# A two-way selective scan: y's state sums two pairs later, eight places for C rows, and a forward half's silus in one group

## The reference

```
def _mamba(xf, Win, conv_w, conv_b, Wx, Wdt, bdt, A_log, D, Wout):
    xz = einsum('blc,ec->ble', xf, Win)
    u, z = split(xz, 2)                       # 256 channels each
    u = silu(causal_conv(u, conv_w) + conv_b) # 4 taps
    x_dbl = einsum('bld,ed->ble', u, Wx)      # dt (8), B (16), C (16)
    delta = softplus(dt @ Wdt.T + bdt)
    dA  = exp(delta * A)                      # 16 states a channel
    dBu = delta * B * u
    h = dA_l * h + dBu_l                      # scan along 16384 positions
    y = sum over n of h[n] * C_l[n]
    y = (y + u * D) * silu(z)
    return y @ Wout.T
x_recon = _mamba(x) + flip(_mamba(flip(x)))   # forward and backward
out = silu(group_norm(x_recon)) + x
```

## Time and profile before

| | us |
|---|---|
| median of 3 runs | 10606.26 |
| lowest and highest | 10604.6 and 10616.05 |
| profiled execution | 10616.89 |
| its span, first to last instruction | 10615.1 |
| first scan of the two-way layer starts | 7012.7 |
| its last scan ends | 10526.2 |

### The profile page before, as it was taken

One profiled execution on the slowest core, in us unless ns is written; L12 is line 12 of the kernel. 1 busy time (PEld: TensorE's weight loads), 2 busy tenths in 40 slices (PEclk: granted clock), 3 DMA queues, 4 the chain that ended last, 5 costly groups with the idle time before them and its releaser, 6 DMA issues. The chain is left out here.

```text
span 10615.1 us, 137498 instructions
## 1 busy us (share of the span) xinstructions
PE 9717.4 (92%) x45956; PEld 5177.6 (49%) x45956; DVE 8515.8 (80%) x8102; ACT 8057.9 (76%) x14637; POOL 5905.9 (56%) x2628
## 2 busy tenths in 40 slices
PE   9999999999899999999999999988888888888885
PEld 6767767677444444444444444433333333333332
DVE  7858858578599999999999411159999999999997
ACT  5646646466488888888888555579999998888885
POOL 0000000000288888888888300058989988889885
PEclk9999999999899999999999999989999999999997
DMA  1000000000145555545555100035555555555556
GB/s 41 0 1 0 0 0 0 0 0 0 61 173 175 175 175 174 177 174 174 176 174 177 66 8 8 8 120 184 186 184 179 187 182 189 184 186 188 183 187 220
DMA packets 335957, 1241.58 MB, mean 117 GB/s; under 512 B 38672, under 2 KB 38800, under 8 KB 331792
## 3 DMA queue, kind: packets, MB, share of 16 engines
q1 hardware_dynamic: 335472, 1235.51, 34.7%
HBM read 1145.18 MB, written 56.62 MB: 113 GB/s over the span
## 5 line engine op out<-in xcount | busy, mean ns | idle before, releaser
L951 POOL TENSOR_TENSOR l_hc<-l_h,l_hc 128x1024 f32<-128x1024 f32 x1024 | 2398.8, 2365 | 451.5 <-DVE l_h L1049 451.0
L1841 POOL TENSOR_TENSOR l_ring<-l_ring 128x1024 f32<-128x1024 f32 x1024 | 2429.7, 2397 | 347.4 <-DVE l_ring L1919 341.3
L1919 DVE TENSOR_TENSOR_SCAN l_ring<-l_ring,l_carry,l_ps 128x1024 f32<-128x1024 f32 x960 | 2200.1, 2333 | 1.3
L688 PE MATMUL l_ps<-l_hc,w_sb 128*128 128x512 f32 x4096 | 1936.4, 595 | 69.1 <-POOL l_hc L951 61.7
L1049 DVE TENSOR_TENSOR_SCAN l_h<-l_decay,l_carry,l_ps 128x1024 f32<-128x1024 f32 x768 | 1760.3, 2334 | 4.3 <-issue 0.4
L1545 PE MATMUL l_ps<-l_ring,w_sb 64*64 64x512 f32 x8192 | 1216.9, 667 | 343.0 <-POOL l_ring L1841 334.4
L116 POOL COPY l_qm<-l_q 128x128 f32 x128 | 82.7, 648 | 2576.4 <-PE l_ps L188 2179.5
L829 ACT ACTIVATE l_decay<-l_delta,w_sb 128x1024 f32<-128x1024 f32 x1024 | 1152.8, 1138 | 168.8 <-DVE l_h L1049 168.6
L1731 ACT ACTIVATE l_xt<-l_duT,l_BT 128x128 f32<-128x128 f32 x4096 | 1246.0, 388 | 0.0
L842 ACT ACTIVATE l_xt<-l_duT,l_BT 128x128 f32<-128x128 f32 x4096 | 1245.9, 388 | 0.0
L212 PE MATMUL l_ps<-l_attnT,l_vT 128*128 128x128 f32 x8192 | 1095.7, 277 | 1.3 <-ACT l_attnT L283 1.3
(11 more groups left out here) (233 smaller groups left out, 15001.6 us busy)
## 6 DMA issues: line engine op xcount, KB each, us to landing
l_hc<-l_rows_dram SPq DMA_DIRECT2D x1024, 512.0 KB, 3.7
l_ring<-l_rows_dram SPq DMA_DIRECT2D x1024, 512.0 KB, 4.8
l_crossed<-l_delta SPq DMA_DIRECT2D x128, 256.0 KB, 5.3
l_gate_dram<-l_gate SPq DMA_DIRECT2D x32, 512.0 KB, 7.1
l_recon_dram<-l_recon SPq DMA_DIRECT2D x32, 512.0 KB, 5.4
l_gate<-l_gate_dram SPq DMA_DIRECT2D x32, 512.0 KB, 6.0
l_xw<-x_dram SPq DMA_DIRECT2D x30, 513.5 KB, 7.3
x_dram<-x SPq DMA_DIRECT2D x16, 512.0 KB, 2.6
```

Of the source, the lines that this page charges most:

```text
L688: ins = nc.tensor.matmul(y_sum[:, half(j)], ident, hc[:, unit % CS, half(j)], start=q == 0, stop=q == S1 - 1)
L951: nc.gpsimd.tensor_tensor(hc[:, unit % CS, :], h[:, unit % HS, :], hc[:, unit % CS, :], ALU.mult).then_inc(hc_done, 1)
L1841: nc.gpsimd.tensor_tensor(hc[:, unit % CS, :], h[:, unit % HS, :], hc[:, unit % CS, :], ALU.mult).then_inc(hc_done, 1)
L1919: nc.vector.tensor_tensor_scan(h[:, unit % HS, order], decay[:, unit % DS, order], x_now[:, order], before, ALU.mult, ALU.add).then_inc(sc ...
```

## The change

It has five parts.

1. TensorE's `add_pair` is called for pair P - 2 instead of P - 1, in the same two places of the iteration. The last two pairs are added after the loop.
2. CS becomes 8: hc has eight slots instead of five.
3. `add_y` of the last half moves from r0 to r1 on VectorE, and `gating` from r1 to r2 on GpSimd.
4. In a forward half ScalarE's r2 copies u (with its bias) and z out of PSUM without silu, into the places of the results (`raw_u`, `raw_z`), and doesn't load a table. In r4 `silu_raw` applies silu to both in place, ahead of the two silus that stood there. The taps of r3 on TensorE wait for the raw copy of z instead of its silu; z in r4 waits for the raw copy of u.
5. `sel` keeps one column for each row (96 by 32), and both broadcasts read it 128 times with step 0.

```diff
-    HS, DS, CS, XS = 4, 4, 5, 4
+    HS, DS, CS, XS = 4, 4, 8, 4
...
-                    ins = nc.tensor.matmul(even_in[:, half(j)], sel[:, r * 128:(r + 1) * 128], stack[:, K % 2, half(j)],
+                    ins = nc.tensor.matmul(even_in[:, half(j)], sel[:, r:r + 1].broadcast_to([PARTS * SEL, 128]), stack[:, K % 2, half(j)],
...
                         if r == 3 and forward(K):
-                            pe.wait_ge(gate_out, 2 * S + 1)
+                            pe.wait_ge(gate_raw, S + 1)
...
                     if r == 4 and forward(K):
-                        pe.wait_ge(u_out, n + 1)
+                        pe.wait_ge(u_raw, S + 1)
                         project_z(S, 1)
...
                     pieces(*divmod(P, PAIRS))
-                    if P:
-                        add_pair(P - 1, 0)
+                    if P > 1:
+                        add_pair(P - 2, 0)
                     if P + 1 < NS * PAIRS:
                         broadcast_B(P + 1)
-                    if P:
-                        add_pair(P - 1, 1)
-                add_pair(NS * PAIRS - 1, 0)
-                add_pair(NS * PAIRS - 1, 1)
+                    if P > 1:
+                        add_pair(P - 2, 1)
+                for P in (NS * PAIRS - 2, NS * PAIRS - 1):
+                    for phase in range(2):
+                        add_pair(P, phase)
...
+                def raw_u(n):
+                    K, e, j = n // 4, n // 2 % 2, n % 2
+                    act.wait_ge(u_mm, n + 1)
+                    at_least(act, y_out, 2 * K + e - 3)
+                    nc.scalar.activation(u[:, K % 2, e, half(j)], [U, V][j], ACT.Identity, bias=col("conv_b", e)).then_inc(u_raw, 1)
+
+                def raw_z(S, j):
+                    act.wait_ge(z_mm, 2 * S + j + 1)
+                    at_least(act, gated_ready, S - 1)
+                    at_least(act, gate_stored, 16 * (S - 1))
+                    nc.scalar.activation(gate[:, S % TI, half(j)], [V, U][j], ACT.Identity).then_inc(gate_raw, 1)
+
+                def silu_raw(S, n):
+                    K, e, j = n // 4, n // 2 % 2, n % 2
+                    own = u[:, K % 2, e, half(j)]
+                    act.wait_ge(u_raw, S + 1)
+                    nc.scalar.activation(own, own, ACT.Silu).then_inc(u_out, 1)
+                    own = gate[:, S % TI, half(0)]
+                    act.wait_ge(gate_raw, S + 1)
+                    nc.scalar.activation(own, own, ACT.Silu).then_inc(gate_out, 1)
...
                     if r == 2 and forward(K):
-                        silu_u(n)
-                        silu_z(S, 0)
-                        exp_set()
+                        raw_u(n)
+                        raw_z(S, 0)
                     if r == 4 and forward(K):
+                        silu_raw(S, n)
                         silu_u(n + 1)
...
-                    if r == 1 and S:
+                    if r == 2 and S:
                         gating(S - 1)
...
-                    if r == 0 and S:
+                    if r == 1 and S:
                         add_y(S - 1)
...
-        sel = ctx.enter_context(nc.sbuf_tensor("sel", [PARTS * SEL, SEL * 128], BF16))
+        sel = ctx.enter_context(nc.sbuf_tensor("sel", [PARTS * SEL, SEL], BF16))
```

More of the change, by code:

```diff
@@ L667, in broadcast_B @@
                 for j in range(2):
-                    ins = nc.tensor.matmul(even_in[:, half(j)], sel[:, k * 128:(k + 1) * 128], stack[:, p, half(j)],
+                    ins = nc.tensor.matmul(even_in[:, half(j)], sel[:, k:k + 1].broadcast_to([PARTS * SEL, 128]), stack[:, p, half(j)],
                                            start=True, stop=True)
@@ L1331, in two_way_scan_layer @@
         x_in = [sem(f"x_in_{i}") for i in range(3)]
-        u_mm = sem("u_mm"); u_out = sem("u_out"); z_mm = sem("z_mm"); gate_out = sem("gate_out")
+        u_mm = sem("u_mm"); u_raw = sem("u_raw"); gate_raw = sem("gate_raw"); u_out = sem("u_out"); z_mm = sem("z_mm"); gate_out = sem("gate_out")
         gate_stored = sem("gate_stored"); gate_loaded = sem("gate_loaded")
@@ L2167, in one_hot_rows @@
 def one_hot_rows():
-    select = _np.zeros((PARTS * SEL, SEL, 128), _np.float32)
-    for a in range(PARTS):
-        for i in range(SEL):
-            select[a * SEL + i, i, :] = 1
-    return select.reshape(PARTS * SEL, SEL * 128).astype(mybir.dt.np(BF16))
+    return _np.concatenate([_np.eye(SEL)] * PARTS).astype(mybir.dt.np(BF16))
 def kernel(**inputs):
```

## The result

The changed kernel took 10408.22 us (median of 4 runs, 10406.57 to 10413.69), the kernel before 10607.49 in the same comparison (10604.6 to 10616.05). The ratio is 0.9815, 95% interval 0.9802 to 0.9827: 199 us faster. The forecast was 10446, the range 10368 to 10532. The profiled execution of the changed kernel took 10406.57 us, span 10404.1. The changed layer ran from 7008.2 to 10316.3, before from 7012.7 to 10526.2: it is 205 us shorter, and the layers ahead of it took what they had taken, within 5 us.

A forecast was written before the change was run, and what follows sets the result against it. A ring of waits with VectorE at its centre, no engine full. Broadcast -168, closing add -25, soft_max +7, ScalarE +26 make -160 from the profiled 10616.9 us: 10457, as median 10446; range 10368 to 10532.

The forecast's parts named there:

- The sums' waits: TensorE's state sums waiting for GpSimd's products: sums two pairs late take these from 334 us to under 30.
- The broadcast's wait: VectorE's input products waiting for TensorE's B broadcast: from 178.4 us to 10, a gain of 168 us.
- add_y: y's closing add on VectorE, moved to r1: mean wait 0.42 us against 0.82, a gain of 25 us.
- soft_max: VectorE's instruction in r3, sharing a port with GpSimd: some 3.6 us against a mean of 3.48, 7 us lost.
- the port's order: In r3, soft_max passes products GpSimd could not yet take when VectorE reached it, so it goes between r3a and r3b.
- rival (a): At r3 the port goes to whoever comes first, so soft_max precedes both products: 56 us less, 10390; chance 0.17.
- The silus' 26 us: Forward chunks: ScalarE busy 102.3 us plus 1.9 of remaining gaps sets 104.2 us a chunk, giving back 26 us.
- the prediction's own sign (below 103): A forward chunk below 103 or above 106 us would say the 1.9 us of remaining ScalarE gaps was wrong.
- The places and weights: Eight C-row places and step-0 weights for TensorE's broadcasts: each counted as 0 us.
- Rival (c): Add at r1 delays GpSimd's chain and soft_max; slower above about 1 us of wait, 10646 at 1.6 us; chance 0.06.

The follow-up runs named there:

- e3_rate: The changed kernel with GpSimd's `input_rate` directly behind `soft_sum` in r3 instead of behind the products of r4: 10390.46 us, ratio to before 0.9793.
- e6_gate1: The changed kernel with GpSimd's `gating` at r1, as before the change, instead of r2: 10423.83 us, ratio to before 0.9823.
- e1_silus: The kernel before with the grouped silus alone (raw copies in r2, silus in r4): 10608.34 us, ratio to before 1.0001.
- e2_sums: The changed kernel with the silus as they were before, all else of the change kept: 10450.9 us, ratio to before 0.9852.
- e5_places: The kernel before with eight C places and the compact step-0 broadcast weights alone: 10608.51 us, ratio to before 0.9998.
- e4_late: The changed kernel with one added VectorE write of 128 x 2048 zeros into an unread tile ahead of each soft_max: 10525.53 us in one run.

## Why the prediction was right in sum and wrong in two steps

**The sums' waits** (334.4 us, forecast under 30) fell to 2.2, of which none is for a product. Right.

**The broadcast's wait** was to fall from 178.4 to 10. It fell to 112.6. This is the step that failed: "Then the broadcast depends on TensorE's own work". I walked TensorE's order in r2, the heaviest pair, and not in r6, where `turn_du` stands ahead of the broadcast and waits for GpSimd's `input_rate`. The view of waits of the kernel before hardly showed it:

```profile
PE l_ps L1501 <- POOL l_du L1826: 5.5, 1, 5.5
```

TensorE came to r6 late itself there, having stood in the sums, so du was ready, but for this one time. The changed kernel took that delay away and met the one behind it, and in the forward halves the lower clock added to its price (1.3 of 1.95 us in the half shown). Gain 66 instead of 168; e3_rate shows 80 of the missing 102 going when du comes earlier.

**add_y** was to gain 25 us and gained 9 (52.5 to 43.9). The waits were put at 0.15 us (e=0) and 0.7 (e=1); they are 0.1 and 1.0 forward, and 1.0 and 0.7 backward.

**soft_max** was to lose 7 and gained 125. The step that failed is the port's order: "Product r3a can be taken by then, product r3b can't. By my reading soft_max goes between". The premise is false in the rows it was read from. Scan r3b stands ahead of soft_max in VectorE's list, so product r3b can be taken before soft_max is reached: 1.33 us before in the earlier trace rows (8134.35 and 8135.68), where soft_max went next all the same, and 1.16 us before in the changed kernel (8110.77 and 8111.93). In the changed kernel soft_max goes ahead of both products in 61 of 63 halves, which is what rival (a) said. The Trainium skill, page "SBUF — State Buffer", section "Who interferes with whom", says "Issue order, not op shape, decides who blocks"; the rows of the changed kernel agree, with 1.43 us for soft_max reached before soft_low ended. Those of e3_rate and e6_gate1 don't by the plain reading: soft_max was reached at 8073.55 and 8118.11, and products that began at 8074.56 and about 8119.8 (half of 4.67 us after 8117.44) went first.

**The silus' 26 us** given back forward: ScalarE takes 101.1 us a chunk against 102.3, and the gap beside it is 1.5 against 1.9; the forward chunk is 102.6 against 104.2, so by the prediction's own sign (below 103) the 1.9 us was too much. Why ScalarE's time fell by 3.9 us a chunk and not 2.7 isn't explained. That ScalarE bounds the forward chunks now and didn't before fits e1_silus and e2_sums, 0 and 43 us for the same edit. Backward 104.8 against 105.2.

**The places and weights** at nothing: e5_places, within its interval of 0.1%. In the changed kernel the products' idle time is 152.6 us, of which 151.7 is for scans, so C rows hardly hold them. Neither part was taken out of the changed kernel by itself.

In sum 66 + 9 + 125 = 200 against 199 measured, where the forecast had 160 from other terms (ScalarE's bound is no term of its own here, since it shows inside VectorE's waits). Two errors, 102 and 132 us, nearly cancel; the forecast's size was partly luck. Rival (a)'s time, 10390, was nearer, with its mechanism for soft_max right and most of its backward gain (2.25 of 3.5 us a chunk) lost to the r6 wait. Rival (c) is not seen: `add_y` waits 0.69 us, under its 1 us.

**What stays open** is what orders soft_max and the products. It is not the lead alone (e6_gate1), and I found no single instant that tells: in e5_places, 15 halves had soft_max reached 0.75 to 0.80 us after a product's start and 1.15 after the end of the scan that the next one needs, and in 13 it went between, in 2 behind. Halves whose instants lie within 50 ns of each other, and not in this order, differ by 2.3 us. What the order costs is measured; why it is so isn't.

## What to carry to other kernels

When a wait is removed, walk every iteration of the engine for the next thing that it waits for, not only the iteration with the most work: here the lighter one had a dependence on a third engine. An edit that frees an engine is to be measured with and without the others, since the same silus were worth 0 and 43 us. And where two engines share a port, read from the trace in which order they took it, and expect that order to change with any edit nearby.

## What the runs showed of the hardware

- After TensorE stood idle for 2.3 us in a forward half of the changed kernel, its clock was granted at 0.50 for about 3 us: eight half-sum matmuls took 1.92 us from start to start instead of 1.02, a broadcast 0.96 instead of 0.54. In e3_rate, with waits of 0.28 and 1.26 us in that place, the same instructions show 1.02 and 0.54. An idle time of 2.58 us in a backward half of the changed kernel brought no drop at all.
- VectorE's write of 2048 four-byte columns took 1.76 us and ran beside a GpSimd product for 1.6 us without slowing it (e4_late, 15 halves).
- soft_max, one instruction of 1024 columns with two inputs in SBUF, took from 1.2 to 7.2 us over these kernels, and the long ones stand beside GpSimd's instructions.
- Weight loads with step 0 took 99 ns, like those of a laid-out table.
